# Audio tower on one core: who scales the second sequence's attention probabilities

## The reference, cut to what matters

```python
h = relu(einsum('blfd,fd,fdk->blk', windows, filt, W) + b_k)      # [32, 248, 64]
n = layernorm(h)
q, k, v = n @ Wq.T + bq, n @ Wk.T + bk, n @ Wv.T + bv
mask = (q[:, :, 0] != 0) & (k[:, :, 0] != 0)                      # one flag for each query row
prob = softmax(where(mask, q @ k.T / 8, -1e9)); prob = where(mask, prob, 0)
h = h + (prob @ v) @ Wo.T + bo
h = h + experts(layernorm(h))                                     # top 2 of 8, weighted
```

## Time and profile before

| what | value |
|---|---|
| median of 3 executions | 307.87 us |
| lowest, highest | 304.54 us, 308.07 us |
| the profiled execution, its own time | 306.96 us |
| its span, first to last instruction | 304.3 us |
| its mean granted TensorE clock | 0.972 |

### The profile page before, as it was taken

The page is one execution under the profiler, slowest core; times in us unless marked ns, Lnnn a source line. Parts: engine busy times, 40 slices in busy tenths (PEclk is TensorE's granted clock), DMA queues, the critical chain, the costliest instruction groups (busy, mean ns, idle before and its releaser), DMA issues.

```text
span 304.3 us, 6060 instructions
## 1 busy us (share of the span) xinstructions
PE 278.6 (92%) x1678; PEld 203.6 (67%) x1678; DVE 232.6 (76%) x888; ACT 235.7 (77%) x545; POOL 107.6 (35%) x101
## 2 busy tenths in 40 slices
PE   8767889999999999999999999999999998888961
PEld 8545567778686867777777868686867765655440
DVE  2575484889797988888888979797888889794743
ACT  2356579898989889888889898989989888676540
POOL 2112113252534352433525153435253423332123
PEclk9989599999999999999999999999999999999797
DMA  5501104336250806252444425170714242333150
GB/s 168 156 18 51 36 3 110 95 94 127 74 151 15 206 4 161 63 145 75 114 112 103 119 73 148 40 183 5 193 29 124 66 101 87 83 106 100 52 152 17
DMA packets 13152, 28.59 MB, mean 94 GB/s; under 512 B 3264, under 2 KB 5568, under 8 KB 13120
## 3 DMA queue, kind: packets, MB, share of 16 engines
q1 hardware_dynamic: 12832, 27.95, 35.4%
q10 hardware_dynamic: 288, 0.28, 0.3%
HBM read 21.86 MB, written 2.29 MB: 79 GB/s over the span
## 4 chain that ended last, share of the span: by engine, by line
PE 41%; DVE 20%; issue 16%; POOL 10%; ACT 6%; DMA 3%; SPq 2%; POOLq 0%; ACTq 0%; DVEq 0%
PE bank_y L901 10%; POOL p L332 10%; PE bank_s L938 5%; PE bank_s L868 4%; PE bank_a L840 4%; PE bank_h L890 3%; DVE acc L578 3%; PE bank_h L891 3%; PE bank_s L906 3%; DVE topi L633 3%; PE bank_b L906 2%; PE bank_s L910 2%; PE bank_s L957 2%; DVE xs L247 2%; ACT xs L410 2%
## 5 line engine op out<-in xcount | busy, mean ns | idle before, releaser
L388 ACT ACTIVATE hid<-bank_h,col 128x496 f32<-128x496 f32 x128 | 82.6, 672 | 8.0 <-PE bank_h L891 3.1
L901 PE MATMUL bank_y<-hid,w_sb 128*64 128x248 f32 x512 | 64.1, 383 | 2.1 <-DVE acc L578 1.9
L890 PE MATMUL bank_h<-xs,w_hi 128*128 128x496 f32 x128 | 56.8, 444 | 1.1 <-ACT hid L388 1.1
L578 DVE SCALAR_TENSOR_TENSOR acc<-bank_y,col,cb 128x248 f32<-128x248 f32 x128 | 53.2, 468 | 4.6 <-DMA cb<-weights 3.7
L332 POOL TENSOR_TENSOR p<-p,rmask 124x496 f32<-124x496 f32 x32 | 35.8, 1119 | 54.4 <-DVE rmask L597 54.3
L901 PEld LDWEIGHTS bank_y<-hid,w_sb 128*64 128x64 f32 x512 | 34.6, 138 | 23.7 <-issue 10.7
L891 PE MATMUL bank_h<-xs,w_lo 128*128 128x496 f32 x128 | 49.8, 389 | 0.0
L256 POOL TENSOR_TENSOR total<-acc 128x496 f32<-128x496 f32 x16 | 20.1, 1256 | 72.8 <-DVE acc L578 72.8
L379 ACT ACTIVATE p<-bank_s,nmax 124x248 f32<-124x248 f32 x64 | 29.0, 466 | 12.8 <-DVE nmax L586 12.8
L890 PEld LDWEIGHTS bank_h<-xs,w_hi 128*128 128x128 f32 x128 | 24.2, 189 | 9.3 <-ACT hid L388 4.4
L840 PE MATMUL bank_a<-x_hi,wconv_hi 128*128 128x504 f32 x64 | 26.7, 502 | 3.6 <-ACT x_hi L444 3.6
(11 more groups left out here) (104 smaller groups left out, 545.8 us busy)
## 6 DMA issues: line engine op xcount, KB each, us to landing
cb<-weights SPq DMA_DIRECT2D x64, 248.0 KB, 3.9
kk<-kk SPq DMA_DIRECT2D x16, 248.0 KB, 3.0
x<-xt SPq DMA_DIRECT2D x15, 256.0 KB, 4.0
out<-h SPq DMA_DIRECT2D x16, 124.0 KB, 2.3
w_sb<-w SPq DMA_DIRECT2D x3, 256.0 KB, 4.0
wtok_sb<-wtok SPq DMA_DIRECT2D x1, 256.0 KB, 2.7
x<-xt ACTq DMA_DIRECT2D x1, 256.0 KB, 3.8
weights<-ct_sb SPq DMA_DIRECT2D x16, 15.5 KB, 1.4
```

The costliest lines, as they stand in the source:

```text
L388: act.activation(hid[2 * (p % 2) + s][:, :], bank_h[s][:, 0:TOK], ACT.Relu, bias=col[:, C_B1 + e:C_B1 + e + 1]).then_inc(hid_ready[s], 1)
L578: last = dve.scalar_tensor_tensor(out=acc[p % 2][:, half], in0=bank_y[p % 2][:, half], scalar=col[:, C_B2 + e:C_B2 + e + 1], in1=cb[:, e, ...
L890: pe.matmul(bank_h[e % 2][:, 0:TOK], w1_hi[:, e, :], xs[m % 2][:, :], start=True, stop=False)
L901: last = pe.matmul(bank_y[p % 2][b * D:b * D + D, s * WIN:(s + 1) * WIN], w2_sb[:, 2 * p + s, :], hid[2 * (p % 2) + s][:, b * WIN:(b + 1) ...
```

## The change

`scale` of POOL is kept for the first sequence alone (as `scale_first`). The second sequence's tile is scaled by ACT, in two activations of 124x248, one for each half, with function Copy and the row's `rmask` as per-partition scale operand. They stand behind `relu(n, 1)` and ahead of `turned(c, 0)` in ACT's iteration. `p_ready` becomes two semaphores, one for each sequence, and the waits of DVE's `recip` and PE's `turn_p` are counted in groups of their own sequence. The wait in `recip(n, b)` is now for the scaling of the same sequence one group earlier.

```diff
-        p_ready = sem("p_ready")
+        p_ready = [sem("p_ready0"), sem("p_ready1")]
...
-            def scale(n, b):
-
-                pool.wait_ge(rm_ready, 2 * n + b + 1)
-                pool.tensor_tensor(p_sb[b][0:HALF, :, :], p_sb[b][0:HALF, :, :],
-                                   rmask[0:HALF, b, :].unsqueeze(2).to_broadcast([HALF, 2, WIN]),
-                                   ALU.mult).then_inc(p_ready, 1)
+            def scale_first(n):
+
+                pool.wait_ge(rm_ready, 2 * n + 1)
+                pool.tensor_tensor(p_sb[0][0:HALF, :, :], p_sb[0][0:HALF, :, :],
+                                   rmask[0:HALF, 0, :].unsqueeze(2).to_broadcast([HALF, 2, WIN]),
+                                   ALU.mult).then_inc(p_ready[0], 1)
...
                 if live(d):
-                    scale(d, 0)
-                    scale(d, 1)
+                    scale_first(d)
...
+            def scale_second(n):
+
+                act.wait_ge(rm_ready, 2 * n + 2)
+                for i in range(2):
+                    last = act.activation(p_sb[1][0:HALF, i, :], p_sb[1][0:HALF, i, :], ACT.Copy,
+                                          scale=rmask[0:HALF, 1, i:i + 1])
+                last.then_inc(p_ready[1], 1)
+
...
                     relu(n, 0)
                     relu(n, 1)
                 if live(c):
+                    scale_second(c)
                     turned(c, 0)
...
             def recip(n, b):
                 dve.wait_ge(ex_ready, 2 * n + b + 1)
-                after(dve, p_ready, 2 * n + b - 1)
+                after(dve, p_ready[b], n)
...
             def turn_p(n, b):
 
-                pe.wait_ge(p_ready, 2 * n + b + 1)
+                pe.wait_ge(p_ready[b], n + 1)
```

## The result

The changed kernel takes 313.16 us (median of four runs, 312.84 to 314.51) against 307.84 us for the kernel before, also four runs: a ratio of 1.021, 95% interval 1.013 to 1.028. It is slower, by 5.3 us; the forecast was 314.9 us and 1.026. When both were timed again, beside the experiments, it was 313.18 against 306.62 us, ratio 1.022 (1.017 to 1.027). Both intervals are clear of 1 and contain 1.02: that the change costs time is shown, that it costs more than 2% is not. The ratios in this document leave out executions more than 1.5% above the fastest of their kernel, which are one of ten of the kernel with the second rmask early, and five of ten of the one that shares the scaling between ACT and POOL, its profiled one among them (309.74 us; over all ten its median is 309.09).

The account below looks back on a forecast made before the run. PE was taken to set the period, with `attend` waiting for ACT's second `turned`. 12 x 0.58 = 7.0 us, plus 0.8 and 0.1, made 7.9 us on 306.96: 314.9 us, range 309.5 to 318.5.

Parts of the forecast that it names:

- What bounds it: PE's program sets the period; `attend` is covered with next to nothing to spare and waits for ACT's second `turned`.
- The cost of the added instructions: Two ACT activations of 124x248 with per-partition scale: 0.49 us each, 0.78 us of ACT's queue, ends 0.60 and 1.04.
- The step from there: One full pass: first `turned` 0.88 us later, second `turned` 0.68, the group behind `attend` 0.58.
- POOL's latency of 0.07: Delay after the second `rmask` is ready, assumed for ACT's start of the scaling: 160.60 to 160.67.
- the loop closes: The next pass's `turn_weights`, on which the second `rmask` waits, shifts too, so 0.58 us is paid once a pass.
- The passes: 12 full passes at 0.58 us give 7.0, second pass 0.8, first, 15th and 16th together 0.1: sum 7.9 us.
- The forecast's own range: 313 to 316.5 us around the forecast of 314.9 us, which was given a chance of 0.50.
- Rival 1: PE keeps what POOL gave up, starting the transposes 0.25 us earlier: 303.7 us, at most 300.5; chance 0.07.
- Rival 2: ACT's activations cost the lower bound, 0.60 us for both; shift 0.40 us a pass, 312.5 us; chance 0.13.
- rival 4: ACT's activations run serially, 1.04 us; shift 0.84 us a pass, 318.4 us; granted clock could also fall; chance 0.14.
- Rival 3: Part of the shift is given back between `attend` and the next `turn_weights`; with half back, 311 us; chance 0.13.
- slower by over 2%: Time above 313.1 us from the profiled execution or 314.0 from the median; chance 0.57, from forecast 0.43 and rival 4 0.14.

Follow-up runs that it names:

- second rmask early: Kernel before, POOL still scaling both sequences, with DVE's masked_recip of the second sequence moved ahead of keep_weights: ratio 1.005, passes of 16.39 us.
- idle copies: Kernel before, POOL still scaling, plus two ACT copies of 124x248 into a scratch tile where the change puts its activations: ratio 1.019, pass 16.76 us.
- dose: Changed kernel with ACT scaling only half 0 of the second tile (POOL half 1), ratio 1.003; or with one more scratch copy on ACT, ratio 1.045.
- kernel that scales on DVE: Changed kernel with the second tile scaled by DVE ahead of keep_weights, multiplying by rsum and mask, without the second masked_recip: 304.15 us, ratio 0.993, passes 16.11 us.

## Why the prediction was right

**What bounds it.** The reading of the earlier trace rows, that `attend` is covered with nothing to spare and that ACT's queue is all but full up to the second `turned`, is what decided. The idle copies show it without any of the change's data flow. The dose shows how little slack the place has: of the 0.87 us by which the first `turned` comes later, 0.24 are covered up to the second one, by ACT's idle time there, 0.10 more by PE, whose matmuls of `attend` started 0.15 us behind their loads before and 0.01 us behind them now, and 0.53 us reach the group behind `attend`; each further activation costs its whole 0.39 us.

**The cost of the added instructions.** No row of before had one. Expected: 0.49 us each and 0.78 for both, with ends of 0.60 and 1.04. Measured: 0.49 us at least and 0.50 in the median (L415, 32 times), 0.90 from the start of the first to the end of the second, and 0.81 us until ACT's next row. Taking the price of a per-partition bias for that of a scale was a guess by likeness, and it was right.

**The step from there.** By the step's own distances from `rmask`:

| | expected, us later | measured |
|---|---|---|
| first `turned` | 0.88 | 0.87 |
| second `turned` | 0.68 | 0.63 |
| loads for `attend` | 0.68 | 0.63 |
| group behind `attend` | 0.58 | 0.53 |
| full pass | 0.58 | 0.52 in the mean, 0.54 for a usual one |

The small miss has three parts: POOL's latency of 0.07 us was taken for ACT, which starts 0.03 us behind `rmask`; the pair holds ACT for 0.81 us and not 0.78; and the spacings of ACT's next three rows came out 0.04 us shorter in all. That the loop closes, and the whole shift comes back once a pass, held to 0.01 us.

**The passes.** 6.21 + 0.74 + 0.03 = 7.0 us in the profiled passes against 7.9 expected. The second pass's 0.8 was 0.74, and of the 0.1 for the end passes 0.03 came. The other 0.8 us is 12 times the difference of a full pass.

**From the passes to the median.** The medians differ by 5.3 us in the first comparison and by 6.6 in the second, so 0.4 to 1.7 us less than the profiled passes give. Part of the 5.3 is scatter of the kernel before: its median was 307.84 over four executions, and 306.3 to 306.6 in three later sets of 11 to 19. Single passes are longer in single executions (17.33 instead of 16.87 in this profile, where PE's L865 waits 0.65 us for the copy of the keys; 16.74 and 16.57 in that of before), and the start-up differs by up to 1.6 us. Which of these makes up the difference was not measured. The forecast's own range, 313 to 316.5, holds the result by 0.16 us only, and some luck is in that: the increase was 5.3 to 6.6 us where 7.9 was forecast, and the forecast was added to the profiled execution's 306.96 us; on the median of 307.87 it would have been 315.8.

**The rivals.** Rival 1 (PE keeps the 0.25 us) was excluded by ACT's queue, and the kernel that scales on DVE shows what it would have been worth with that queue left alone: 16.11 instead of 16.33 us a pass. Rival 2's number, 312.5 us, is nearer to the 313.16 measured than the forecast's 314.9, so the time alone doesn't decide between them; the pair's 0.81 us does, where rival 2 needed 0.60 and rival 4 1.04. The lower clock that rival 4 thought possible was not there, 1.00 in the full passes. Rival 3 (part given back later in the pass) is not seen in the passes: 0.53 us at the group behind `attend`, 0.52 to 0.54 in the pass. I had given slower by over 2% a chance of 0.57 with the forecast near the line; the ratios of 1.021 and 1.022 are as near to it.

**What the prediction did not see** is that POOL's multiplications hold DVE. It changed no term, since in the kernel before and in the changed one DVE has nothing in its way there; it would have been wrong for the kernel with the early `rmask`, where I expected 0.990 and got 1.005.

## What to carry to other kernels

A stall that stands in the chain with 10% isn't worth 10%: removed at little other cost it gave 0.22 us a pass, and nothing where the change made the next wait in line later. Look one instruction past it, at who releases that one, and at what would be queued ahead of it. Work that is moved to an engine with 23% idle time costs most of its duration if it lands in the stretch where that engine has next to none: 0.54 of 0.81 us a pass here, and all of what came on top. In a gap of DVE the same work fitted, and 0.2 us a pass was won. A dose in one place (nothing for the result, only time) tests such a reading directly.

## What the runs showed of the hardware

A DVE instruction that reads two SBUF tiles is held until POOL's running multiplication is through, also where DVE has 124x2 elements to do: 0.77 us instead of 0.16 for `rmask`, 1.03 instead of 0.41 us for `ts`, beside POOL multiplications of 1.01 us each. A `tensor_scalar` with two per-partition operands, 124x248 and one SBUF tile, was held as well, 0.90 us beside POOL against 0.40 behind it in the same pair (with one such operand, away from POOL, it took 0.35); what in it makes it wait for POOL was not tried. DVE instructions that read one tile in PSUM and one in SBUF were not held: `hsum` (L674), two of them from 162.62, take 0.82 us beside POOL's L259 (162.01 to 163.25). The other way round POOL's multiplication of 124x496 takes 1.01 us beside DVE's idle time, and 1.24 where DVE's L247 starts 0.04 us ahead of it. From the order of time of the kernel before, POOL, then DVE:

```profile
158.60 1.01 POOL L332 TENSOR_TENSOR p<-p,rmask 124x496 f32<-124x496 f32 x1 [1.77 <-DVE rmask L597]
```

```profile
160.63 0.41 DVE L247 TENSOR_TENSOR ts<-xn,ts 64x248 fp32r<-64x248 f32 x1
```

An ACT activation with a per-partition scale takes 0.49 us for 248 columns, 0.09 more than L460 of the same size without one, which is also what a per-partition bias adds at 496 columns (0.67 against 0.58). The next one can start 0.39 to 0.41 us behind its start.
